# Fused image-text layer on one core: values of two images made ahead, shifts inside the rotation, a fourth up bank, counts one step later, a second routed place loaded in advance

## What is computed

```python
h = tok(x)                     # 16 images, 36 patches of 768 each: layernorm, @ W + bias, layernorm, + position; class row first
h = concat([h, txt], axis=1)   # 16 sequences of 1 + 36 + 32 = 69 rows of 256
n = layernorm(h)
q, k, v = n @ wq.T, n @ wk.T, n @ wv.T
h = h + softmax(rotate(q) @ rotate(k).T / 16) @ v
n = layernorm(h)
out = h + n + gelu(n @ shared_up) @ shared_down
p = softmax(n @ router_w)      # 8 experts; the two largest probabilities are the gates
out += sum over the two chosen experts e of p[e] * gelu(n @ up[e]) @ down[e]
```

## Time and profile before

| what | us |
|---|---|
| runs (three) | 316.44, 318.51, 317.61; median 317.61 |
| the profiled execution, whole | 316.77 |
| its span, first to last instruction | 314.8 |
| PE busy in the span | 294.7 |
| POOL / DVE / ACT busy | 209.7 / 157.7 / 143.4 |

### The profile page before, as it was taken

One profiled execution on the slowest core, in us unless ns is written; L12 is line 12 of the kernel. 1 busy time (PEld: TensorE's weight loads), 2 busy tenths in 40 slices (PEclk: granted clock), 3 DMA queues, 4 the chain that ended last, 5 costly groups with the idle time before them and its releaser, 6 DMA issues.

```text
span 314.8 us, 6647 instructions
## 1 busy us (share of the span) xinstructions
PE 294.7 (94%) x2040; PEld 267.3 (85%) x2041; DVE 157.7 (50%) x399; ACT 143.4 (46%) x323; POOL 209.7 (67%) x176
## 2 busy tenths in 40 slices
PE   8999799898998999989999999999999999999970
PEld 6678789777997999879999999999999999999860
DVE  3898888897459995423322332322332322333310
ACT  3696242869595445435343433343433344433400
POOL 3687095388830047499888988988987998255541
PEclk9999999999999999999999999999999999999996
DMA  7998113133643227574552552652355342324432
GB/s 239 299 177 277 47 52 134 43 95 131 221 163 105 90 75 205 177 251 152 183 169 69 181 183 39 195 179 70 133 168 167 51 66 33 50 33 49 53 35 31
DMA packets 21990, 39.90 MB, mean 127 GB/s; under 512 B 2978, under 2 KB 18292, under 8 KB 19668
## 3 DMA queue, kind: packets, MB, share of 16 engines
q0 software_dynamic: 7456, 25.43, 30.0%
q1 hardware_dynamic: 14228, 14.03, 15.1%
q10 hardware_dynamic: 288, 0.20, 0.3%
HBM read 28.85 MB, written 6.93 MB: 114 GB/s over the span
## 4 chain that ended last, share of the span: by engine, by line
POOL 35%; issue 15%; PE 14%; DMA 13%; DVE 12%; ACT 6%; POOLq 3%; DVEq 0%; ACTq 0%
POOL ring L473 15%; DMA out_tokens<-xy_all,dest 12%; POOL ring L472 7%; POOL xy_all L633 6%; POOL out_tokens L643 4%; PE ps L944 3%; PE ps L915 2%; POOL stage L462 2%; POOLq L640 2%; DVE ps L1348 2%; DVE qk L1347 2%; PE ps L1054 1%; DVE hid L1474 1%; PE ps L1056 1%; PE ps L1055 1%
## 5 line engine op out<-in xcount | busy, mean ns | idle before, releaser
L473 POOL TENSOR_TENSOR ring<-stage,ring 128x512 fp32r<-128x512 f32 (+2 forms) x30 | 76.1, 2538 | 2.5
L1672 DVE TENSOR_TENSOR hgT<-ps,hgT 128x512 fp32r<-128x512 f32 x50 | 32.2, 686 | 73.0 <-ACT hgT L905 73.0
L1054 PE MATMUL ps<-ring,hgT 128*128 x200 | 58.3, 292 | 2.1 <-DVE xy_all L1678 1.5
L643 POOL DMA_INDIRECT out_tokens<-xy_all,dest x25 | 39.5, 1582 | 26.9 <-DMA out_tokens<-xy_all,dest 15.1
L1055 PE MATMUL ps<-ring,hgT 128*128 x200 | 56.3, 282 | 0.0
L1056 PE MATMUL ps<-ring,hgT 128*128 x200 | 56.3, 282 | 0.0
L897 ACT ACTIVATE hg<-ps 128x512 f32<-128x512 f32 x50 | 30.0, 599 | 47.0 <-PE ps L1056 47.0
L633 POOL DMA_INDIRECT xy_all<-normalized_tokens,dest x25 | 24.5, 981 | 31.5 <-DVE dest L1621 24.2
L1054 PE MATMUL ps<-ring,xgT 128*128 x100 | 40.9, 409 | 0.8 <-ACT hg L897 0.8
L1054 PEld LDWEIGHTS ps<-ring,hgT 128*128 128x128 f32 x200 | 37.7, 188 | 2.6 <-issue 2.6
L1056 PE MATMUL ps<-ring,xgT 128*128 x100 | 39.5, 395 | 0.0
(11 more groups left out here) (209 smaller groups left out, 583.8 us busy)
## 6 DMA issues: line engine op xcount, KB each, us to landing
stage<-in_w_up POOLq DMA_DIRECT2D x9, 1024.0 KB
stage<-in_w_dn POOLq DMA_DIRECT2D x9, 1024.0 KB
xg<-xy_all SPq DMA_DIRECT2D x25, 128.0 KB
xp<-in_patches SPq DMA_DIRECT2D x4, 384.0 KB, 7.5
normalized_tokens<-hn SPq DMA_DIRECT2D x4, 276.0 KB
residual_tokens<-h SPq DMA_DIRECT2D x4, 276.0 KB
ring<-in_tok_w SPq DMA_DIRECT2D x1, 768.0 KB, 6.0
base<-residual_tokens SPq DMA_DIRECT2D x3, 256.0 KB, 2.7
```

What stands on the lines that cost most here:

```text
L473: return nc.gpsimd.tensor_tensor(lo, stage[:, part, c0:c1], hi.bitcast(F32), ALU.subtract)
L643: pool.indirect_dma_start(out, bass.IndirectOffsetOnAxis(ap=dest[:, t:t + 1].bitcast(U32), axis=0), xy_all[:, t, :], None, compute_op=ALU. ...
L1054: nc.tensor.matmul(o, a[0], b[0], start=n == 0, stop=False)
L1672: v.tensor_tensor(hgT[:, c, 1, 4 * half:4 * half + 4, :], ps[:, turned_bank + half, :].rearrange("p (k t) -> p k t", k=4), hgT[:, c, 0, 4 ...
```

## The change

- Token stage (DVE): the first half of the statistics of tile 1 goes ahead of `tok_shift(0)`.
- `values_ahead`: PE makes the values of images 0 and 1 of group 1 into bank 1 before scores(0), where the turning of token tile 7 stood; that moves between the two halves of `attention_qk(1)`, and `attention_v(1)` makes two images only. ACT copies the two images by `keep_ahead`. Tiles 7 and 8 swap banks; ACT's and DVE's order around them follows. `attention_out(0)` waits for tile 8's low part only ahead of its third image.
- DVE: cosine and sine products become two helpers, and `flat_shift(g - 1)` stands between them. The first rotation stands ahead of `attention_bias(3)`.
- ACT: `flat_base(1)` leaves the attention loop (it stood ahead of the last `attention_exp`) and stands behind `shared_act(4)`, ahead of `flat_high(3)`.
- `shared_up(2)` goes into bank 5 and ahead of `attention_out(3)`; from step 8 there are four up banks 4, 7, 2, 3.
- PE's counting sums stand behind step 10, not 9; the tables behind step 16, not 15. DVE: `shared_end(0, 3)` and `shared_parts(10)` go ahead of the wait for the sums; the second `shared_end` ahead of `expert_low(2)`.
- The places of the first two routed tiles are loaded in advance.

```diff
-        TURN_BANK = (0, 1, 6, 7, 0, 1, 0, 1, 0)
+        TURN_BANK = (0, 1, 6, 7, 0, 1, 0, 0, 1)
-        LANES, TABLE, TABLE_AT = 128, 256, 16
+        LANES, TABLE, TABLE_AT = 128, 256, 17
-        up_bank = [2 + n % 2 for n in range(8)] + [(4, 2, 3)[(n - 8) % 3] for n in range(8, NSG * KF - 1)] + [2]
+        up_bank = [2, 3, 5, 3, 2, 3, 2, 3] + [(4, 7, 2, 3)[(n - 8) % 4] for n in range(8, NSG * KF)]
...
+            def keep_ahead():
+                act.wait_ge(v_ahead, 1)
+                nc.scalar.activation(vv[:, 1, 0:2, :].rearrange("p b d -> p (b d)"), ps[0:SEQ, 1, :], ACT.Copy).then_inc(v_kept, 1)
...
             attention_copy(6)
+            attention_values(0)
+            keep_ahead()
             attention_norm(3)
-            attention_values(0)
-            attention_copy(7)
-            attention_norm(4)
             for g in range(NG - 1):
                 attention_exp(g)
                 if g == 0:
+                    attention_copy(7)
+                    attention_norm(4)
                     attention_copy(8)
...
                 if g >= 1:
                     flat_high(g - 1)
-                    flat_base(g - 1)
+                    if g < NG - 2:
+                        flat_base(g - 1)
...
             shared_act(4, 5)
+            flat_base(NG - 3)
             flat_high(3)
...
+                    if g == 1 and eo == 0:
+                        attention_transposes(7)
...
-                for b in (2, 3, 0, 1):
+                for b in (2, 3) if g == 1 else (2, 3, 0, 1):
...
+            def values_ahead():
+
+                te.wait_ge(a_low, NG + LAST_TILE[1] + 1)
+                for b in range(2):
+                    last = values_of(1, b, 1)
+                last.then_inc(v_ahead, 1)
...
-                te.wait_ge(a_low, NTURN)
+                te.wait_ge(a_low, NTURN if g else NTURN - 1)
...
+                    if g == 0 and b == 2:
+                        te.wait_ge(a_low, NTURN)
...
-                    elif n >= 2:
+                    elif n >= 8:
                         te.wait_ge(f_lo, NG)
+                        if up_bank[n] == 7:
+                            te.wait_ge(r_sub, 1)
...
+                        if n == 0 and down_bank[j] in up_bank[0:4]:
+                            te.wait_ge(s_lo, up_bank.index(down_bank[j]) + 1)
...
             attention_probs(NG - 1)
+            shared_up(2, 3)
             attention_out(NG - 1)
-            shared_up(2, 4)
+            shared_up(3, 4)
...
-            shared_steps(7, 10)
+            shared_steps(7, 11)
...
-            shared_steps(10, TABLE_AT)
+            shared_steps(11, TABLE_AT)
...
-            first_turn = te.value_load(eplace[0:1, 0:1], min_val=4, max_val=4 * NX + RING)
+            first_turns = [te.value_load(eplace[0:1, n:n + 1], min_val=4, max_val=4 * NX + RING) for n in range(2)]
...
+            attention_cos(0)
+            attention_sin()
+            attention_rope(0)
             attention_bias(3)
-            attention_turn(0)
-            attention_rope(0)
...
                 attention_sums(g)
+                if g == 0:
+                    attention_low(7)
                 if g + 1 < NG:
-                    attention_turn(g + 1)
+                    attention_cos(g + 1)
                 else:
                     attention_probs(g)
-                if g == 0:
-                    attention_low(8)
                 if g >= 1:
                     flat_shift(g - 1)
                 if g + 1 < NG:
+                    attention_sin()
+                    if g == 0:
+                        attention_low(8)
                     attention_rope(g + 1)
...
             shared_parts(8, 10)
+            shared_end(0, SG)
+            shared_parts(10, 11)
             dve.wait_ge(r_prefix, 1)
...
-            shared_parts(10, 11)
-            shared_end(0, SG)
...
-            shared_parts(14, TABLE_AT)
+            shared_parts(14, 16)
```

More of the change, by code:

```diff
@@ L741, in attention_values @@
                     act.wait_ge(a_pv, g - 1)
-                nc.scalar.activation(vv[:, g % 2, :, :].rearrange("p (a b) d -> p a (b d)", a=2),
-                                     ps[0:SEQ, 6:8, :], ACT.Copy).then_inc(a_vs, 1)
+                first = 1 if g == 1 else 0
+                nc.scalar.activation(vv[:, g % 2, 2 * first:, :].rearrange("p (a b) d -> p a (b d)", a=2 - first),
+                                     ps[0:SEQ, 6 + first:8, :], ACT.Copy).then_inc(a_vs, 1)
+            def keep_ahead():
+                act.wait_ge(v_ahead, 1)
+                nc.scalar.activation(vv[:, 1, 0:2, :].rearrange("p b d -> p (b d)"), ps[0:SEQ, 1, :], ACT.Copy).then_inc(v_kept, 1)
             def attention_exp(g):
@@ L993, in attention_v, with values_of @@
                     te.wait_ge(a_exp, g)
-                for b in (2, 3, 0, 1):
+                for b in (2, 3) if g == 1 else (2, 3, 0, 1):
                     if g >= 1 and b == 0:
                         te.wait_ge(a_pTs, g)
-                    last = split_product(ps[0:SEQ, 6 + b // 2, D * (b % 2):D * (b % 2 + 1)],
-                                         [([hT_n[:, v, c, GT * g + SEQ * b:GT * g + SEQ * (b + 1)] for v in range(2)],
-                                           [wv2[:, v, c, :] for v in range(2)]) for c in range(KD)])
+                    last = values_of(g, b, 6 + b // 2)
                 last.then_inc(a_v, 1)
+            def values_of(g, b, bank):
+                return split_product(ps[0:SEQ, bank, D * (b % 2):D * (b % 2 + 1)],
+                                     [([hT_n[:, v, c, GT * g + SEQ * b:GT * g + SEQ * (b + 1)] for v in range(2)],
+                                       [wv2[:, v, c, :] for v in range(2)]) for c in range(KD)])
+            def values_ahead():
[3 more added lines that the diff above has]
+                last.then_inc(v_ahead, 1)
             def attention_scores(g):
@@ L1196, in step @@
                     te.wait_ge(x_lo, s + 2)
-                    if first and s == -1:
-                        turn = first_turn
+                    if first and s < 1:
+                        turn = first_turns[s + 1]
                     else:
@@ L1248, in link, with tok_stats_half, tok_stats_sum @@
                 dve.wait_ge(s_dve, link_count[0])
-            def tok_stats(i):
-                dve.wait_ge(patches_in[i], 16)
-                r = TROWS[i]
-                for j in range(2):
-                    last = v.bn_stats(tst[0:r, i, 6 * j:6 * j + 6], xp[0:r, i, 384 * j:384 * (j + 1)])
-                link(last)
-                v.bn_aggr(tmv[0:r, i, :], tst[0:r, i, :]).then_inc(t_stats, 1)
+            def tok_stats_half(i, j):
+                if j == 0:
+                    dve.wait_ge(patches_in[i], 16)
+                r = TROWS[i]
+                return v.bn_stats(tst[0:r, i, 6 * j:6 * j + 6], xp[0:r, i, 384 * j:384 * (j + 1)])
+            def tok_stats_sum(i):
+                r = TROWS[i]
+                v.bn_aggr(tmv[0:r, i, :], tst[0:r, i, :]).then_inc(t_stats, 1)
+            def tok_stats(i):
+                tok_stats_half(i, 0)
+                link(tok_stats_half(i, 1))
+                tok_stats_sum(i)
             def tok_turned(i):
@@ L1645, in expert_low @@
                     last.then_inc(w_free, 1)
[L1647 removed]
+            shared_parts(16, 17)
             for n in range(8):
+                if n == 2:
+                    shared_end(SG, 2 * SG)
                 expert_low(n)
                 if n < 2:
[L1651 to L1655 removed]
+                    shared_parts(17 + n, 18 + n)
+                elif n > 2:
+                    shared_parts(16 + n, 17 + n)
             def x_low(s, c, first=False):
```

21 lines of the change are left out of this document (10 added, 11 removed).

## The result

The changed kernel takes 320.98 us (median of 5 runs, 320.32 to 321.13) where the kernel before took 317.15 us beside it (5 runs, 315.34 to 318.51): 1.0109 of before, 95% interval 1.0062 to 1.0156. It is slower by about one per cent. Its profiled execution took 321.05 us with a span of 319.0 us.

What follows compares the result with a forecast made beforehand. PE, busy 94% of the span, was taken as the bound. The late copy's +2.7, less 0.5 (place) and 0.3 (start), gave +1.9: 318.7 us profiled, 319.5 for the median, range 312.2 to 322.2.

Steps and rivals of the forecast that it cites:

- the clock: Rival: PE's clock falls in the gap between up(19) and down(16), costing 1.9 us, for 321.4 us; chance 0.28.
- The chain of copies: SP's queue behind `flat_base(1)`: base(1) at 83.45, then keeps and loads in order, all landed at 111.9 to 116.
- The sum: Whole kernel: +2.7 at K = 115, less 0.5 (place) and 0.3 (start): +1.9; without the late copy, 5.4 us shorter.
- the gains ahead of the copy: PE from attention through the shared steps: gaps removed, so the shared steps would end 4.6 us earlier.
- K: Time when all four residual copies that ACT's `expert_high(0)` needs have landed: taken as 115, wanted by ACT at 103.5.
- The two gaps: PE idle 3 us just before down(15) and up(19), then 5.2 us before down(16) at K + 9.3.
- the place loaded ahead: Routed tiles' start: most of PE's wait of 0.76 us at 139.03 goes; 0.5 taken, bounds 0 and 0.76.
- the wait of 0.54 for ScalarE: PE's wait for ACT's normalized rows in attention, claimed to go because `flat_shift` comes 1.32 us earlier.
- The wait of 1.05 for `flat_low(1)`: PE at `shared_up(0)`: asks at 66.8, but `flat_low(1)`, behind `attention_end(2)` on DVE, is ready at 67.8.
- the late residual: `flat_base(1)` moved behind `shared_act(4)`: f_base(1) at about 83.45 instead of 71.2, holding SP's queue; PE +2.7 at K = 115.
- the fourth bank: Shared up products on PE: takes away the wait of 0.67 us at 128.91.
- the later counts: PE's counting sums one step of 2.07 us later lose their 0.79 us wait, and down(8) its 0.5.

Runs made afterwards that it cites:

- e3: The kernel before with only `flat_base(1)` moved behind `shared_act(4)`: 322.5 us, 1.0148 of before.
- e9: The changed kernel with the last two copies of the residual tokens issued one behind the other, ahead of the loads waiting for them: 316.82 us, 1.0018 of before.
- e4: The changed kernel with idle PE products in both gaps, ahead of down(15) and down(16): 320.27 us, 1.0095 of before.
- e2: The changed kernel with SP issuing keep_normed(2) and keep_normed(3) ahead of keep_base(1): 318.15 us, 1.0013 of before.
- e1: The changed kernel with `flat_base(1)` put back ahead of the last attention exp: 314.7 us, 0.9927 of before.
- e8: e1 with the last two residual copies issued together and DVE's second `shared_end` one step earlier: 313.9 us, 0.9875 of before.
- e6: e1 with counts at step 10, table at 16 and DVE's order around them as before: 315.27 us, 0.9903 of before.
- e7: e1 with the values of two images and the rotation's shifts back in their old places: 317.22 us, 0.9957 of before.
- e10: e8 with the third and fourth routed tiles transposed straight from the gathered rows, without SP's copies: 313.29 us, 0.9890 of before.
- e12: e11 with `flat_shift` behind the sine product again, leaving only the values made ahead: 316.04 us, 0.9985 of before.
- e11: The kernel before with only the values of two images made ahead and the shifts inside the rotation: 313.76 us, 0.9923 of before.
- e5: e1 with the up products on three banks again: 314.48 us, 0.9896 of before.

## Why the prediction was right, and where it was not

The forecast was 319.5 us, +1.9 on the kernel before; the measurement is 320.98, +3.8. The mechanism was the one forecast, and the steps can be checked one by one. The size of the loss was not: the one term that made the difference is the clock, below.

**The chain of copies.** Forecast: base(1) at 83.45, its landing at 88.65, the next load at 107, the last copy landed at 115. Measured: 83.87, 89.67, 107.54, 114.74. The last number is partly luck. The copy alone took 5.80 us and not 5.2, and the last one 6.26 and not 7.3. The weight load that was to run through the three copies was nearly over at 93 us (70 of its packets from 91 to 93, 6 from 93 to 95, none after), yet these copies took nearly what the forecast allowed with it. (The forecast's 3 engines of 16 would be 18.8%; the 20.4% in the earlier trace rows is a little more, which nothing here explains.) e3 and e9 show that this chain is the cause: doing the move alone brings the loss, and taking one wait out of the chain takes away half of it. The sum did not need the gains ahead of the copy to be right: once ACT waits for the copy, down(16) follows from K alone.

**From the copy to PE.** With K = 114.74 the forecast's own terms give part(15) ended at 116.7 (measured 116.74), `dest` at 118.7 (118.57) and down(16) at K + 9.3 = 124.04 (124.05). The two gaps were forecast at 3 and 5.2 us and measured at 2.46 and 3.55, while down(16) came where it should: the slow clock, which the forecast had left out, stretched down(15) and up(19) into the second gap.

**The clock.** The forecast left it out, as a rival of chance 0.28 with a price of 1.9 us. It happened on top. PE should have been K - 112.3 = 2.4 us late before the routed tiles; it was 5.1 late, and the missing 2.7 is what e4 shows for that stretch. The rival took its measure from the 3.6 us that PE had been idle at the end of before. Here the clock fell inside a gap of 2.46 us already (0.86 in the window from 115 to 117), while in e2 a gap of 2.43 us ahead of 141.52 passed at 1.00. In these runs the length of a gap alone does not tell whether the clock falls. This step, the slow clock priced at nothing in the sum, is the one that failed; it measured 2.7 us, and the rival's own price was 1.9. The profiled executions lie 4.3 us apart where +1.9 was forecast: 2.7 from the clock and 0.35 from POOL's additions, less what the routed tiles gave back beyond the forecast (PE 5.10 late at the first of them, 3.92 at its last result, so 1.18 given back; 0.5 was forecast, for the place loaded ahead).

**The gains.** 4.6 us ahead was forecast for PE before the copy bites. At the tables PE was 1.81 us earlier with one step of 2.07 us more behind it, 3.88. The gain in the attention was overrated: scores(1) was to be 1.4 us earlier and was 0.83 (47.69 before, 46.86 now); scores(3) was to be 3.4 us earlier and was 2.17 (68.82 before, 66.65 now). The waits of group 0 cost what was said, but in group 1 the wait of 0.54 for ScalarE was not removed; one of 0.75 for VectorE's rotation took its place. The wait of 1.05 for `flat_low(1)` came as forecast (67.8 - 66.8).

**Half of e1's expected gain.** The sum promised 5.4 us without the late residual, and e1 won 2.3. One part is the clock, in the profiled executions. Between 68.7 and 97 us e1 and e8 do the same work from the same start (first shared product at 68.71 and 68.72), and the counting sums start here, in e1 and in e8:

```profile
97.78 0.27 PE L1203 MATMUL ps<-rcum,counters 128*128 128x80 f32 x1
```

```profile
96.27 0.27 PE L1207 MATMUL ps<-rcum,counters 128*128 128x80 f32 x1
```

The 1.51 us between them is one stretch of slow clock, beside no gap, in these windows of e1 and of e8:

```profile
78.00:82.00 4.00, 4.00 (x21) 4.00 (x21) 1.26 (x4) 2.39 (x5) 3.74 (x6) 0.61 0.91 329
```

```profile
78.00:82.00 4.00, 4.00 (x30) 4.00 (x30) 1.53 (x5) 2.80 (x6) 3.74 (x6) 1.00 0.92 326
```

Of e1's runs, the two with a mean clock of 0.992 took 312.76 and 313.17 us, near the expected 312.5; but one with 0.994 took 315.47, so the clock is not all of it. A second part stands in e1's routed stage. Its first routed up product ran 2.79 us earlier than before (132.07 against 134.86), which is 4.3 with the 1.5 us added, close to the 4.6 of the sum. Then PE waited 0.73 us for a copy of gathered rows at 135.71, about what the place loaded ahead had won. What the other runs of e1 lost is in no trace. And the parts that were priced at 0.5 to 1 us each as gaps removed (the fourth bank, the later counts) brought nothing measurable.

## What to carry to other kernels

Before moving a step later, list what it feeds in an in-order queue, and add up all that stands behind it there, with each landing that the queue waits for in turn; here one residual of 2.07 us, moved 12 us later, held a transfer for 7 us and the engine behind it for 10. Where a queue waits for a copy before it issues the next, issuing the copies together (with a semaphore for each that something waits for) can recover part of that for nothing; here it was half. Gaps removed from the busiest engine don't add up: of this change's edits the fourth bank and the later counts closed gaps of half a microsecond and more and brought nothing that the runs can tell. The values made ahead and the early shift together brought all of the measured gain, and the values without the shift hardly any.

## What the hardware showed that was not expected

**A slow copy beside a weight load.** A copy over 69 partitions moves 71 packets per us when alone. The DMA queues in e2, from 92 to 95 us, with a copy pending on q1 the whole time:

```profile
q0 software_dynamic: 77, 0.52, 46.5%
q1 hardware_dynamic: 34, 0.03, 3.3%
```

34 packets in 3 us, 11 per us. In the first of these microseconds the load had the engines (52 packets, 100.6%), and the copy moved 25; in the next two the load had only 19 and 6 packets left, and the copy moved 3 and 6. At 96 us it was back at 71. The Trainium skill (DMA: Bandwidth & Descriptors, Queues, rings and completion order) says that each DMA engine takes turns between its queues packet by packet. The trace agrees that both move in the same microseconds, but does not settle whether turns explain a copy at a tenth of its rate: in the last two microseconds the load's packets took 27.0% and 12.1% of the time of 16 engines, that is about 4 and 2 engines' worth, the copy takes about 3 when alone (20.4% of 16), and the view does not tell whether they were the same ones. What held the copy is not shown here, and it was seen in one execution.

**The clock falls where no gap is.** In e1, e2, e4, e6, e7, e10 and e12 the granted clock of the window from 78 to 82 us was 0.57 to 0.78 with PE busy throughout; in before, the changed kernel, e3, e8, e9 and e11 it was 1.00 there. (In e5 it was 0.64, but there the clock had fallen at 74 us, just behind the gap of 2.23.) e1 and e8 have the same work in that stretch, and the fall cost 1.5 us between them. The mean clock also differs between runs of one kernel, from 0.980 to 0.994 in e1, so a single profile can't rank two such kernels. What sets the fall off is not shown.
